# Blanking the rows behind each expert's end while the last pairs run, and splitting the gate and up weights in the last full pair

## The reference

```python
x = x + attention(layernorm(x), ctx)                  # 16 heads of 64, W_qkv, W_out, b_out
xt = layernorm(x).reshape(4096, 128)
logits = xt @ Wg.T + bg
top_vals, top_idx = top_k(logits, 2);  rw = softmax(top_vals)
gu = xt @ Wgu[e] + bgu[e];  gate, up = gu[..., ::2], gu[..., 1::2]
gate = minimum(gate, 7);    up = clip(up, -7, 7)
out_e = ((up + 1) * gate * sigmoid(1.702 * gate)) @ Wd[e] + bd[e]
x = x + sum over the token's two experts of rw * out_e
```

## Time and profile before

| | us |
|---|---|
| median of three runs | 735.1 (729.92 to 735.44) |
| the profiled execution | 730.95 |
| its span, first to last instruction | 729.2 |
| PE busy | 608.5 (83%) |
| DVE busy | 589.5 (81%) |
| ACT busy | 503.2 (69%) |
| POOL busy | 464.3 (64%) |

### The profile page before, as it was taken

How to read it: one execution, slowest core, us unless ns; L and a number is a source line. 1 busy time by engine, 2 the same in 40 slices (tenths; PEclk the granted TensorE clock), 3 DMA queues, 4 the chain that set the end, 5 groups by cost and what they waited for, 6 DMA issues and landing times.

```text
span 729.2 us, 21626 instructions
## 1 busy us (share of the span) xinstructions
PE 608.5 (83%) x6857; PEld 464.7 (64%) x6858; DVE 589.5 (81%) x1613; ACT 503.2 (69%) x1397; POOL 464.3 (64%) x506
## 2 busy tenths in 40 slices
PE   0769899989989898898988989898955999999920
PEld 0447678867877677786877878686842555555510
DVE  5886899899999999999999989987984366666615
ACT  0667799878888888888888878796850366666510
POOL 2163666879688796877879678785245066657640
PEclk9987999999999999999999999999975999999965
DMA  8600300000000000000000000000004233323129
GB/s 228 182 1 2 116 3 2 17 2 15 15 0 15 0 15 7 7 15 0 15 4 11 15 0 15 0 17 15 10 16 90 63 90 83 85 81 83 42 69 284
DMA packets 42308, 31.43 MB, mean 43 GB/s; under 512 B 6196, under 2 KB 38348, under 8 KB 42260
## 3 DMA queue, kind: packets, MB, share of 16 engines
q1 hardware_dynamic: 27700, 17.45, 9.2%
q0 software_dynamic: 4704, 8.67, 3.6%
q10 hardware_dynamic: 9856, 4.70, 2.4%
HBM read 19.09 MB, written 12.76 MB: 44 GB/s over the span
## 4 chain that ended last, share of the span: by engine, by line
PE 31%; DVE 26%; POOL 17%; issue 15%; ACT 6%; DMA 3%; SPq 1%; ACTq 1%; POOLq 1%; DVEq 0%
PE bank L1005 7%; POOL places L607 7%; PE bank L1007 5%; PE bank L1006 5%; PE bank L1163 4%; POOL results L620 3%; POOL qk L565 3%; DVE xhat L679 3%; PE bank L1088 3%; PE bank L1171 3%; POOL qk L568 3%; DVE qmax L823 2%; DVE picked L869 2%; DVE oT L819 2%; DMA ctx_sb<-results 2%
## 5 line engine op out<-in xcount | busy, mean ns | idle before, releaser
L565 POOL TENSOR_TENSOR qk<-qkf,zeros 128x512 f16<-128x512 f32 x90 | 114.2, 1269 | 74.4 <-ACT qkf L398 74.1
L568 POOL TENSOR_TENSOR qk<-qkf,qk 128x512 f16<-128x512 f32 x120 | 140.1, 1167 | 21.0 <-ACT qkf L398 13.6
L455 ACT ACTIVATE probs<-bank,nbias 128x128 f32<-128x128 f32 x512 | 146.0, 368 | 5.2
L620 POOL DMA_INDIRECT results<-z,stage x80 | 78.7, 984 | 64.5 <-ACT z L490 48.9
L847 DVE TENSOR_TENSOR pT<-bank,pT 128x512 f16<-128x512 f32 x128 | 87.3, 682 | 14.7 <-ACT pT L464 13.4
L1005 PE MATMUL bank<-qk 64*128 64x128 f16 x512 | 94.3, 220 | 3.1 <-POOL qk L568 1.8
L1006 PE MATMUL bank<-qk 64*128 64x128 f16 x512 | 93.0, 218 | 0.0
L1007 PE MATMUL bank<-qk 64*128 64x128 f16 x512 | 93.0, 218 | 0.0
L1088 PE MATMUL bank<-ident,probs 128*128 128x128 f32 x512 | 85.8, 291 | 2.7 <-DVE pT L847 2.6
L823 DVE TENSOR_REDUCE qmax<-bank 128x4 f32<-128x512 f32 x128 | 86.8, 679 | 0.9 <-PE bank L1007 0.8
L398 ACT ACTIVATE qkf<-bank 128x512 f32<-128x512 f32 x120 | 72.3, 602 | 18.6 <-POOL qk L568 13.2
(11 more groups left out here) (199 smaller groups left out, 1948.6 us busy)
## 6 DMA issues: line engine op xcount, KB each, us to landing
stage<-places SPq DMA_DIRECT2D x80, 65.0 KB, 1.9
ctx_sb<-results SPq DMA_DIRECT2D x16, 256.0 KB, 5.5
ctx_sb<-in_ctx_dram ACTq DMA_DIRECT2D x4, 512.0 KB, 10.7
stage<-in_L_ffn_Wgu_dram SPq DMA_DIRECT2D x1, 2048.0 KB, 8.5
out_dram<-x_sb ACTq DMA_DIRECT2D x8, 256.0 KB, 5.3
stage<-in_L_xattn_W_qkv_dram SPq DMA_DIRECT2D x3, 512.0 KB, 6.7
results<-z,stage POOLq DMA_INDIRECT x80
places<-payload,slots POOLq DMA_INDIRECT x64, 2.4
```

The costliest lines, as they stand in the source:

```text
L455: last = nc.scalar.activation(probs[:, b, k, :], score_bank[b][:, k * P:(k + 1) * P], ACT.Exp, bias=nbias[:, b, k:k + 1], scale=exp_scale)
L565: nc.gpsimd.tensor_tensor(qk_item(par, t, HI), src, zeros[:, :].rearrange("p (i n) -> p i n", i=2), ALU.add).then_inc(s["qk_high"], 1)
L568: nc.gpsimd.tensor_tensor(qk_item(par, t, LO), src, qk_item(par, t, HI), ALU.subtract).then_inc(s["qk_split"], 1)
L620: nc.gpsimd.indirect_dma_start(out=results, out_offset=bass.IndirectOffsetOnAxis(ap=to, axis=0), in_=z[:, (u - 5) % NZ, t, :], in_offset=None,
```

## The change

- DVE copies the ends of that moment to `ends` in iteration 14, at the end of step 5, when pairs 0 to 12 are counted, and no longer after the last pair.
- SP alone then writes, for each of the 16 experts, 7 x 128 blank rows from that end on: the last three pairs have 768 tokens, so at most 6 x 128 more rows per expert, plus a block. `clear_ends` and its calls on ACT and POOL are gone, and so is the semaphore `pool_cleared`.
- POOL waits, before the scatters of pairs 13, 14 and 15 (iterations 15, 16, 17), for all 16 blankings. SP's wait for them ahead of the first load is gone.
- The eight chunks of the gate and up weights go to the eight steps of iteration 15, the last one with scores, from iterations 16 and 17.
- The fill ahead of the first block has 24 matmuls, not 52.

```diff
@@ gu_chunk
-            at = p * STEPS + r - PAIRS * STEPS - 1 if isinstance(p, int) else -1
-            return at if 0 <= at < 8 else None
+            return r if isinstance(p, int) and p == PAIRS - 1 else None
@@
-        def clear_ends(eng, experts, done="cleared"):
-
-            for e in experts:
-                first = eng.value_load(ends[0:1, e:e + 1], min_val=e * ROOM, max_val=e * ROOM + TOK)
-                eng.dma_start(places[bass.ds(first, P), :], blank[:, :]).then_inc(s[done], 16)
+        LATE = 3
+        CLEAR = LATE * 2 + 1
@@ sync
             sp.wait_ge(s["ends_ok"], 1)
-            clear_ends(sp, range(0, 7))
+            for e in range(NE):
+                first = sp.value_load(ends[0:1, e:e + 1], min_val=e * ROOM, max_val=e * ROOM + TOK - (CLEAR - 1) * P)
+                sp.dma_start(places[bass.ds(first, CLEAR * P), :].rearrange("(k p) w -> p k w", p=P),
+                             blank[:, :].unsqueeze(1).to_broadcast([P, CLEAR, ROW])).then_inc(s["cleared"], 16)
             for par in range(2):
                 sp.wait_ge(scattered[par], 64 * (PAIRS // 2))
-            sp.wait_ge(s["cleared"], 16 * 13)
-            sp.wait_ge(s["pool_cleared"], 16 * 3)
             sp.wait_ge(s["blank_in"], 16)
@@ scalar
             over_pairs(act, steps)
-            act.wait_ge(s["ends_ok"], 1)
-            act.wait_ge(s["blank_ok"], 2)
-            clear_ends(act, range(7, 13))
@@ gpsimd
                         wait_alone(pool, "ylow", p * 2 - 2)
+                        if isinstance(p, int) and p - 2 >= PAIRS - LATE:
+                            pool.wait_ge(s["cleared"], 16 * NE)
                         for j in range(2):
@@
             over_pairs(pool, steps)
-            pool.wait_ge(s["ends_ok"], 1)
-            clear_ends(pool, range(13, NE), "pool_cleared")
@@ vector
                     if isinstance(p, int):
                         weights_low(p, r)
+                    if isinstance(p, int) and (p, r) == (PAIRS + 1 - LATE, 5):
+                        sofar = next_place[0:1, (p + 1) % 2, :]
+                        nc.vector.tensor_copy(ends[:, :], sofar).then_inc(s["ends_ok"], 1)
@@
-            nc.vector.tensor_copy(ends[:, :], final[0:1, :]).then_inc(s["ends_ok"], 1)
@@ tensor
-            fill(banks[2], 52)
+            fill(banks[2], 24)
```

More of the change, by code:

```diff
@@ L184, in xattn_moe_kernel @@
         place_ok picked_ok slots_ok denom_ok wgt_ok
-        table_cols table_mm table_ok ends_ok cleared pool_cleared
+        table_cols table_mm table_ok ends_ok cleared
         t_mm t_ok gu_mm gate_ok up_ok sig_ok glu_ok h_ok ht_mm ht_hi ht_lo d_mm z_ok
```

## The result

The changed kernel takes 743.8 us (median of six runs, 740.0 to 745.54) and the kernel before, run beside it, 732.56 (six runs, 729.92 to 735.44). The ratio is 1.0143, with a 95% interval of 1.0101 to 1.0185: 10.5 us slower by the ratio, 11.2 by the medians. The forecast was 4 us faster, and the rival "the blanks are late" said 741 in the terms of the profiled execution, 10 us slower, with a chance of 0.17 for any loss and of 0.08 for one over 1%, which is what came.

What follows compares the result with a forecast made beforehand. The fill was taken to end last before the first expert block, with SP's wait for blanked rows second. -6.0 + 5.3 + 0.1 - 2.9 - 0.5 = -4.0 us: 730.95 to 727.0 profiled, median 729.5, range 724 to 737.

Steps and rivals of the forecast that it cites:

- the blanks are late: Rival: blank rows reach DRAM at 163 GB/s, done at 555.1, 10 us slower, 741; chance 0.17 for loss, 0.08 over 1%.
- The seam, -6.0: Before the first expert block: 28 fewer fill matmuls at 0.2135 us each save 6.0 us; the fill still ends last.
- the 1.4 us that I gave to the fill alone: Before block 0: shortening only the fill, with SP's wait for blanked rows kept, would bring 1.4 us.
- Iteration 15, +5.3: Iteration 15: eight weight chunks on a full DVE cost 0.66 us each, 5.3 us together; bounds 4.2 and 6.5.
- the two collisions with POOL: Iteration 15: two moved chunks meet POOL at work, adding at most 2 x 0.6 us, within the upper bound 6.5.
- Iterations 16 and 17, -2.9: Iterations 16 and 17 without the chunks: 2.2 us from `oT` rounds, 0.4 before the last residual, 0.25 before the logits.
- The -0.5 for `picked`: End of the routing: `picked` may start ahead of POOL's L598 and spare its delay; -0.5 us, between 0 and -1.1.
- The blanking, 0: SP's 7.45 MB of blank rows at 280 GB/s are done at 536.0, before anyone waits, so cost 0.
- a cover until 541.1: Blanks done by 541.1 delay nobody, which takes 235 GB/s; each microsecond later costs one.
- the rival of dearer chunks: Iteration 15: chunks cost 1.0 us a step, 8.0 in all, net -1.3, 729.7 against 730.95; chance 0.18.
- the seam of 3.7: Rival before block 0: clock rises later or first loads are slower, gain only 3.7, net -1.7, 729.3; chance 0.1.
- The rival in which iteration 15 absorbs more: Iteration 15 costs +4.2 and the drain gives all: -6.0 us in total, 725; chance 0.15.

## Why the prediction was wrong, step by step

- *The seam, -6.0.* Right. The fill went from 13.90 to 7.05 us, -6.9. Part of that is the luck of this pair of profiles: on chips of this speed a fill of 52 took 13.2 to 13.9 us in three of them and one of 24 took 6.5 to 7.9 in six, depending on how soon the granted clock rose. That fill and blanking together bring more than the fill alone was said; but the 1.4 us that I gave to the fill alone did not come (1.0001), since the clock falls back in the gap, and that I had not seen.
- *Iteration 15, +5.3.* Right in kind, a little high: +5.0 in the changed kernel, +4.0 with the chunks alone. Of the two collisions with POOL that the sum allowed for only the first came, and it was harder than bounded: the first chunk took 1.97 us instead of 0.74, the second ran undisturbed. POOL's timeline beside it:

```profile
514.11 1.28 POOL L559 TENSOR_TENSOR qk<-qkf,zeros 128x512 f16<-128x512 f32 x1
515.47 1.50 POOL L562 TENSOR_TENSOR qk<-qkf,qk 128x512 f16<-128x512 f32 x1
```

  The chunk was held for 1.2 us, as long as L559 ran, and L562, which began while the chunk still ran, took 1.50 instead of 1.16. The Trainium skill's SBUF — State Buffer, section Who interferes with whom, has one of the two block the other for a whole instruction; the trace agrees here, and my 0.6 per collision was too low a bound for this one. In four other profiles with the chunks in iteration 15, on chips of this speed, it took 1.33 to 1.56.
- *Iterations 16 and 17, -2.9.* Right: -2.5 to the last residual and -0.4 behind `y`. The -0.5 for `picked` did not come: it took 1.30 us still (before: 1.36), again beside POOL's L592.
- *The blanking, 0.* This is the step that failed, with +16.5 us. Its form was right: a cover until 541.1, each microsecond behind it costs one. POOL came to the scatter at 535.25 and the blanks were done at 559.2; 559.2 - 541.1 = 18.1, and since iteration 15 began 1.5 us later in this profile, the cover ended 1.5 later too: 16.6 against the 16.5 found. What was wrong is one number, the rate: 280 GB/s was put in, 164 came. I had two rows, 280 and 163 GB/s, and chose the first as the nearest, "since here the writes have the engines to themselves". But the first row moved 512-byte rows, and the second the very rows in question, 520 bytes into `places`, only on three queues and beside scatters. I put its slowness down to the company and not to the rows. The runs show that the pieces decide: 162 GB/s in another order of addresses, from 192 to 297 by padding them to 576 bytes, 374 in pieces of 3640. What makes the 520-byte rows slow is not settled; with few of them under way one took less than half of the engine time.
- *The rivals.* The late blanks were worked out at 163 GB/s as done at 555.1, 10 us slower, 741; measured 559.2 and 743.8. Of those 4.1 us 1.9 are the later first issue (509.3 for 507.4). Everything was there but the weight: 0.08 for a loss over 1%. With the blanks out of the way the changed kernel is 5.0 us faster than before (0.9932), and the chunks alone cost 0.9, so the rival of dearer chunks falls; so does the seam of 3.7. The rival in which iteration 15 absorbs more (-6.0 in all) is not told apart from the forecast's -4.0 by 3.3 to 6.7.

## What to carry to other kernels

When a transfer is moved to where it must be hidden, price it by the row that has the same bytes per piece and the same destination, whatever else was going on there, and not by the row with the same company. Here a DMA share of 1.2 to 1.3 at 160 to 190 GB/s went with pieces that were slow: then try larger or padded ones, before shifting anything in time. The share alone says little, since the padded rows had 1.14 at 297 GB/s. And a filler that keeps the clock up can be shortened only as far as what it waits for really comes sooner.

## What the runs showed of the hardware

Writing rows to DRAM from SP's queue, with the queue full, went at 162 to 192 GB/s with rows of 520 bytes, which begin at multiples of 8 within `places`, and at 297 to 305 with rows of 576 bytes at multiples of 64. Pieces of 3640 bytes at multiples of 8 went at 351 to 374, with SP's pace as the limit. In the first case the packets' summed time was 1.2 to 1.3 of the engines' time, in the others 0.93 to 1.14; with fewer 520-byte rows under way it was 0.62 at 179 GB/s. The Trainium skill, DMA: Bandwidth & Descriptors, section How a descriptor splits into AXI transactions, says that a piece that does not start at a multiple of 256 bytes is begun at the boundary below, and that the bytes before its start cost extra beats. It says this of reads. Pieces of 576 bytes mostly do not start at such a multiple in `places` either and were fast there, so that rule does not tell the two apart. PE's clock, after the 4.76 us of idleness between fill and block 0, was at its lower level for most of the next 5 us (0.52 in 570 to 575 us), and 14 matmuls of 512 columns took 5.34 us instead of 3.19.
